# Four-layer graph network on one core: other waits, products and transfer sizes around the node steps

## What is computed

```python
edge_index = jnp.stack([src, dst])
h = jnp.maximum(_layernorm(x, axis=-1), 0.0)
x = x + _L0_gnn_ref(h, node_vec1, src, dst, edge_attr_4, edge_attr_12, ...)
...
x = x + _L2_gnn_ref(h, edge_attr_3, edge_attr_64, ...)
h = jnp.maximum(_layernorm(x, axis=-1), 0.0)
x = x + _L3_gnn_ref(h, node_vec1, edge_attr_4, edge_attr_8, ..., src, dst, 16)
return x
```

```python
skip_s = s @ W_skip0
skip_v = jnp.einsum('nmi,mk->nki', v, W_skip1)
s = s @ W_nl0
v = jnp.einsum('nmi,mk->nki', v, W_nl1)
w = jax.nn.relu(edge_feature @ W_fc1) @ W_fc2
xs = s[dst]
xv = v[dst]
...
tp = jnp.concatenate([out0a, out0b, ...], axis=-1)
agg = jax.ops.segment_sum(tp, src, num_segments=N) / DENOM
out_s = agg_s @ W_out_s + skip_s
out_v = jnp.einsum('nmi,mk->nki', agg_v, W_out_v) + skip_v
```

## Time and profile before

| | us |
|---|---|
| median of three runs | 5989.67 |
| the profiled execution | 5993.88 |
| its span | 5992.1 |
| PE busy | 4809.9 (80%) |
| DVE busy | 4674.1 (78%) |
| POOL busy | 4116.6 (69%) |
| ACT busy | 3747.7 (63%) |
| DMA traffic | 488.43 MB, mean 82 GB/s |

### The profile page before, as it was taken

The page is one execution under the profiler, slowest core; times in us unless marked ns, Lnnn a source line. Parts: engine busy times, 40 slices in busy tenths (PEclk is TensorE's granted clock), DMA queues, the critical chain, the costliest instruction groups (busy, mean ns, idle before and its releaser), DMA issues. The chain is left out here.

```text
span 5992.1 us, 143928 instructions
## 1 busy us (share of the span) xinstructions
PE 4809.9 (80%) x37273; PEld 4178.0 (70%) x37273; DVE 4674.1 (78%) x14217; ACT 3747.7 (63%) x13000; POOL 4116.6 (69%) x4263
## 2 busy tenths in 40 slices
PE   0078787777788888888889899999999878888886
PEld 0047777777777777777777688888888757777775
DVE  9947777777777777777776499999999569999996
ACT  0046666666665666666665477777777468888884
POOL 1677777777777777777777377777776247777772
PEclk9999999999999999999999899999999879999998
DMA  6432333333333333333333233333333223333332
GB/s 195 112 83 72 75 74 76 75 75 75 75 80 82 76 75 75 76 73 75 74 81 77 81 82 81 81 81 80 82 81 76 72 70 84 84 84 85 82 80 62
DMA packets 599937, 488.43 MB, mean 82 GB/s; under 512 B 308280, under 2 KB 526134, under 8 KB 599447
## 3 DMA queue, kind: packets, MB, share of 16 engines
q0 software_dynamic: 195056, 322.11, 21.1%
q1 hardware_dynamic: 366138, 137.90, 10.0%
q10 hardware_dynamic: 38637, 27.25, 1.5%
HBM read 410.81 MB, written 75.56 MB: 81 GB/s over the span
## 5 line engine op out<-in xcount | busy, mean ns | idle before, releaser
L896 PE MATMUL PS<-WK 128*128 128x123 f32 (+1 forms) x21632 | 2677.5, 283 | 264.8 <-issue 208.3
L896 PEld LDWEIGHTS PS<-WK 128*128 128x128 f32 (+1 forms) x21632 | 2565.5, 196 | 443.7 <-issue 416.9
L1136 ACT ACTIVATE WK<-WK 128x64 f32<-128x64 f32 x9984 | 2470.9, 336 | 308.2 <-DVE WK L1601 302.8
L657 POOL DMA_INDIRECT WK<-HT,WK x2080 | 2024.0, 973 | 807.3 <-issue 702.4
L657 POOL DMA_INDIRECT ACC<-HT,WK x832 | 801.3, 963 | 254.8 <-issue 242.4
L576 POOL DMA_INDIRECT TB<-WK x718 | 719.9, 1003 | 247.2 <-issue 233.1
L1105 ACT ACTIVATE WK<-PS 100x512 f32<-100x512 f32 x420 | 246.9, 588 | 689.4 <-PE PS L862 686.2
L879 PE MATMUL PS<-F,WK 100*128 100x192 f32 x3360 | 657.5, 339 | 11.8 <-DVE WK L1619 9.2
L879 PEld LDWEIGHTS PS<-F,WK 100*128 100x128 f32 x3360 | 541.0, 191 | 68.2 <-DVE WK L1619 40.7
L884 PE MATMUL PS<-F,WK 64*128 64x224 f32 (+1 forms) x3360 | 413.3, 365 | 161.2 <-DVE WK L1619 131.5
L657 POOL DMA_INDIRECT WOA<-HT,WK x416 | 425.2, 1022 | 169.7 <-issue 118.9
(11 more groups left out here) (234 smaller groups left out, 6606.2 us busy)
## 6 DMA issues: line engine op xcount, KB each, us to landing
WK<-TA SPq DMA_DIRECT2D x638, 72.0 KB, 1.9
WK<-HT,WK POOLq DMA_INDIRECT x2080
WK<-TB SPq DMA_DIRECT2D x214, 144.0 KB
WK<-in_ea SPq DMA_DIRECT2D x23, 612.0 KB
TA<-WK POOLq DMA_DIRECT2D x23, 612.0 KB, 7.6
ACC<-HT,WK POOLq DMA_INDIRECT x832
WK<-in_eb SPq DMA_DIRECT2D x400, 32.0 KB
HT<-WK ACTq DMA_DIRECT2D x153, 76.9 KB
```

Of the source, the lines that this page charges most:

```text
L657: eng.indirect_dma_start(out=GB[l][u % 4][:, t, :], out_offset=None, in_=HT[:, :], in_offset=bass.IndirectOffsetOnAxis(ap=idx[:, t, vc:vc ...
L896: m = eng.matmul(psA[q][0:ch, k * BN:(k + 1) * BN], ms[:, t, k * ch:(k + 1) * ch], OH[q][:, t, :], start=(t == 0), stop=(t == G - 1))
L1136: m = eng.activation(m4[:, t, 96 + vb * c:160 + vb * c], m4[:, t, 96:160] if l == 2 else TW[l][q][:, t, :], ACT.Copy, scale=tb[:, t, y1 + ...
```

## The change

- **Waits.** In the edge loops PE's feature transposes, its first edge product (layers 2 and 3) and its sum of messages wait on fewer semaphores.
- **Products of layer 2.** In `mnode` four products of 64, 96, 96 and 96 columns become two of 192 columns. 32 zero columns are put between the two scalar weights, and the second product overwrites what they leave.
- **Filling products.** In the last ten tiles of the node steps 1 to 2 and 2 to 3, where `mout` has no tile left, PE multiplies the identity by output weights (`warm`). Nothing reads the result.
- **Clearing.** Layer 0's `ACC` is cleared in 51 pieces by ACT during node step 0 (`first`).
- **TB.** 166 columns in the prologue, 96 in node step 0 to 1, 120 in node step 1 to 2 (before 174, 104, 104).
- **Skip rows.** Pieces of four tiles in four buffers in place of eight in two.
- **SP.** The eight first loads of layer 3 are issued between the stores of tiles 2, 5, ..., 23, not ahead of all.
- **Start of layer 3.** The evacuation buffers of that node step lie elsewhere (`EV3`), and DVE no longer waits for the last store before it splits layer 3's first features.
- **POOL.** In layers 0 and 1 a group's gathers are issued ahead of its scatter, and the wait on `e.A` moves with them.
- Two semaphores of the prologue's sort are merged into others.

The diff, cut:

```diff
-SB0, SB1 = 174, 104
+SB0, SB1, SB2 = 166, 96, 120
...
-NEV, SKB = 5, 8
+NEV, SKB, NSK = 5, 4, 4
...
-        EVL = [EV0, EV1, EV2, EV2]
-        SK = [WK[0:BN, 4480 + i * SKB * 192:4480 + (i + 1) * SKB * 192].rearrange("p (j d) -> p j d", j=SKB) for i in range(2)]
+        EV3 = [WK[0:BN, 5848 + i * 352:6200 + i * 352] for i in range(NEV)]
+        EVL = [EV0, EV1, EV2, EV3]
+        SK = [WK[0:BN, o:o + SKB * 192].rearrange("p (j d) -> p j d", j=SKB) for o in (3328, 4096, 4864, 7616)]
...
-        loads += [(WS[2][:, 0:64], w["L2_gnn_W_nl0"]), (WS[2][:, 64:160], w["L2_gnn_W_skip0"])]
+        loads += [(WS[2][:, 0:64], w["L2_gnn_W_nl0"]), (WS[2][:, 96:192], w["L2_gnn_W_skip0"])]
...
                 if l == 3:
-                    for u in range(8):
-                        load(0, u)
                     for j in range(NB):
                         store(eng, 3, j)
+                        if j % 3 == 2 and j < 24:
+                            load(0, j // 3)
...
+            eng.memset(WS[2][:, 64:96], 0.0).then_inc(s_wz, 1)
...
                     eng.wait_ge(s_bl[u % 4], i * 64 + (u // 4 * 32 + 64 * NT0 * l + 32))
                     eng.sem_inc(s_sep, 1)
-                    if u % 2 == 0:
-                        follow(i, u)
                     place(TB, lambda q: st[:, q, POSC:POSC + 1].bitcast(I32), st, s_bs[u % 4])
 
                 eng.wait_ge(s_az, l + 1)
                 if l < 2:
                     with eng.Fori(0, NT0) as i:
                         for u in range(8):
+                            gather(i, u, u % 2 == 0)
                             scatter(i, u)
-                            gather(i, u)
                 with eng.Fori(NT0 if l < 2 else 0, n) as i:
                     for u in range(8):
...
-                        eng.dma_start(SK[q % 2][:, 0:w, :],
+                        eng.dma_start(SK[q % NSK][:, 0:w, :],
                                       SC[q * SKB * BN:(q * SKB + w) * BN, 0:192].rearrange("(j p) d -> p j d", p=BN))\
-                           .then_inc(s_sk[q % 2], 16)
...
                     eng.wait_ge(s_le, 3)
-                    skip_rows(0)
-                    skip_rows(1)
+                    for q in range(NSK):
...
                     m = p["nch"] * BN
                     for j in range(NB):
                         eng.wait_ge(s_oo, l * NB + j + 1)
                         x = eng.memset(ACC[:, j * m:(j + 1) * m], 0.0)
-                        if j and j % SKB == 0 and j + SKB < NB:
+                        if j and j % SKB == 0 and j + (NSK - 1) * SKB < NB:
                             eng.wait_ge(s_o, j)
-                            skip_rows(j // SKB + 1)
+                            skip_rows(j // SKB + NSK - 1)
                     x.then_inc(s_az, 1)
...
-                        eng.matmul(o[:, 0:64], t[0:64, 0, 0:BN], WS[2][:, 0:64], start=True, stop=True)
-                        eng.matmul(o[:, 160:256], t[0:64, 0, 0:BN], WS[2][:, 64:160], start=True, stop=True)
-                        eng.matmul(o[:, 64:160], t[0:96, 1, 0:BN], KV[2][:, 0:96], start=True, stop=True)
-                        m = eng.matmul(o[:, 256:352], t[0:96, 1, 0:BN], KV[2][:, 96:192], start=True, stop=True)
+                        s2 = o[:, 0:320].rearrange("p (a f) -> p a f", a=2)[:, :, 0:96]
+                        v2 = o[:, 64:448].rearrange("p (a f) -> p a f", a=2)[:, :, 0:96]
+                        eng.matmul(s2, t[0:64, 0, 0:BN], WS[2][:, :], start=True, stop=True)
+                        m = eng.matmul(v2, t[0:96, 1, 0:BN], KV[2][:, :], start=True, stop=True)
...
+                def warm(t):
+
+                    if lo == 2:
+                        eng.wait_ge(s_o, min(NB, t - 3))
+                    else:
+                        eng.wait_ge(s_xo, lo * NB + min(NB, t - 3))
+                    eng.matmul(psO[t % 4][0:BN, 0:WO[lo].shape[2]], ident[0:ch, 0:BN], WO[lo][:, 0, :], start=True, stop=True)
...
+                        elif lo:
+                            warm(t)
...
-                    if not isinstance(i, int) or g >= 2:
+                    if isinstance(i, int) and g >= 2 or not isinstance(i, int) and (l < 2 or k == 0):
                         eng.wait_ge(e.E, i * 8 + (g - k))
-                    if l >= 2 and (not isinstance(i, int) or g >= 4):
-                        eng.wait_ge(e.S, i * 8 + (g - k - 2))
+                    if l >= 2 and isinstance(i, int) and g >= 4:
+                        eng.wait_ge(e.S, g - k - 2)
...
-                    eng.wait_ge(e.E, i * 8 + (g - q + 2 if l >= 2 else g + 1))
-                    if not (isinstance(i, int) and g - (q if l >= 2 else 0) == 0):
-                        eng.wait_ge(e.S, i * 8 + (g - q if l >= 2 else g))
-                    eng.sem_inc(s_sep, 1)
+                    if l < 2 or isinstance(i, int):
+                        eng.wait_ge(e.E, i * 8 + (g - q + 2 if l >= 2 else g + 1))
+                        if not (isinstance(i, int) and g - (q if l >= 2 else 0) == 0):
+                            eng.wait_ge(e.S, i * 8 + (g - q if l >= 2 else g))
+                        eng.sem_inc(s_sep, 1)
...
                 def edge_a(i, u):
                     q = u % 2
                     ms = MS[l][q][:, 0:G * nm].rearrange("p (t f) -> p t f", t=G)
-                    eng.wait_ge(e.M, i * 8 + (u + 9))
                     eng.wait_ge(e.N, i * 8 + (u + 9))
                     eng.wait_ge(e.V, i * 8 + (u + 2))
...
                     eng.wait_ge(s_oo, lo * NB + j + 1)
                     m = LAYERS[lo]["nch"] * BN
+                    x = eng.activation(ACC[:, j * m:(j + 1) * m], ZERO[:, :].to_broadcast([128, m]), ACT.Copy)
+                    if j == NB - 1:
+                        x.then_inc(s_az, 1)
+
+                def first(j):
+                    if j == 0:
+                        eng.wait_ge(s_ws, 1)
+                        eng.wait_ge(s_px[0], 16)
+                        eng.wait_ge(s_px[1], 16)
+                        eng.wait_ge(s_wz, 6)
+                    m = LAYERS[0]["nch"] * BN
                     x = eng.activation(ACC[:, j * m:(j + 1) * m], ZERO[:, :].to_broadcast([128, m]), ACT.Copy)
                     if j == NB - 1:
                         x.then_inc(s_az, 1)
...
+                    if lo is None and t < NB:
+                        first(t)
...
-            eng.wait_ge(s_px[0], 16)
-            eng.wait_ge(s_px[1], 16)
-            eng.wait_ge(s_wz, 5)
-            m = NB * LAYERS[0]["nch"] * BN
-            eng.activation(ACC[:, 0:m], ZERO[:, :].to_broadcast([128, m]), ACT.Copy).then_inc(s_az, 1)
...
-                        eng.wait_ge(s_sk[j // SKB % 2], 16 * (j // SKB // 2 + 1))
+                        eng.wait_ge(s_sk[j // SKB % NSK], 16 * (j // SKB // NSK + 1))
                         if j >= 2:
                             eng.wait_ge(s_xo, base + j - 1)
-                        eng.tensor_tensor(OO[j % 2], o[:, 0:192], SK[j // SKB % 2][:, j % SKB, :], ALU.add).then_inc(s_o, 1)
...
                     eng.wait_ge(s_xn, NB * (l + 1))
-                    for x in range(NEV):
-                        eng.wait_ge(s_hd[x], all_stored(l)[x])
                     if l == 3:
                         v(eng.memset(twf[:, 0:576], 0.0))
                         w_()
+                    else:
+                        for x in range(NEV):
+                            eng.wait_ge(s_hd[x], all_stored(l)[x])
```

More of the change, by code:

```diff
@@ L279, in program @@
         s_oo, s_xo, s_wz, s_wo, s_ox, s_tl = (sem(n) for n in ("s_oo", "s_xo", "s_wz", "s_wo", "s_ox", "s_tl"))
-        s_sk, s_ske, s_skl = [sem(f"s_sk{i}") for i in range(2)], sem("s_ske"), sem("s_skl")
+        s_sk, s_ske, s_skl = [sem(f"s_sk{i}") for i in range(NSK)], sem("s_ske"), sem("s_skl")
         s_o, s_sg, s_hz = sem("s_o"), sem("s_sg"), sem("s_hz")
@@ L709, in _ @@
             eng.wait_ge(s_cf, 1)
-            eng.matmul(psO[2][:, 0:1], ONE, CF, start=True, stop=True).then_inc(s_cg, 1)
+            eng.matmul(psO[2][:, 0:1], ONE, CF, start=True, stop=True).then_inc(s_cp, 1)
             for b in range(NKEYS):
```

28 lines of the change are left out of this document (15 added, 13 removed).

## The result

The changed kernel is slower: 6012.05 us in the median of 17 runs (5999.98 to 6018.2), beside 5995.88 us for the kernel before in as many (5982.89 to 6000.08). The ratio is 1.0026 with a 95% interval of 1.0019 to 1.0034. Forecast were 5955 us and a gain. The profiled execution took 6011.65 us.

What follows compares the result with a forecast made beforehand. POOL's DMA issue was taken to bound layers 0, 1 and 3, and PE layer 2, leaving gains in prologue and node steps: -11 - 2 - 10 + 0 - 12 = -35 us, giving 5955 us against the median; range 5925 to 5978.

Steps and rivals of the forecast that it cites:

- new order of gather and scatter: Edge loops of layers 0 and 1: worth nothing, 0 us, since POOL issues as many DMAs at the same pace.
- The slower rival: Node step 2 to 3: more skip-row pieces in flight stall SP's stores, giving 6001 us; chance 0.05.
- Prologue: Start of layer 0: clearing in pieces and fewer TB columns start it near 428, not 439; -11 us (-13 to -7).
- Node step 0 to 1: Between layers 0 and 1: 8 fewer TB columns let the stores land a little sooner; -2 us (-3 to 0).
- Node step 1 to 2: Between layers 1 and 2: merged products save 0.44 to 0.48 us a tile, partly limited by ACT's stores; -10 us (-18 to 0).
- stores and loads swallow the node steps: Rival, node steps: ACT's queue limits step 1 to 2, loads take back step 2 to 3's head gain; 5970 us, chance 0.24.
- the clock holds: Rival, last ten tiles: filling products keep PE at full clock, saving up to 10 us; 5945 us, chance 0.07.
- Layer 2: Layer 2's edge loop: removing PE's waits gains 0 us, at the far end 32 us.
- waits were dear: Rival, layer 2: removing PE's waits gains 32 us as well, giving 5924 us; chance 0.11.
- Node step 2 to 3 and layer 3: From layer 2's end into layer 3: smaller skip pieces and an earlier DVE start give -12 us (-25 to +5).
- The head: Start of node step 2 to 3: four-tile skip pieces land after 9 to 11 us, not 19; -9 us (-13 to -3).
- SP's queue is full: Node step 2 to 3: SP's stores bind, so layer 3's interleaved loads add 8 us (0 to +10).

Runs made afterwards that it cites:

- f1: The changed kernel with POOL's scatter put back ahead of the gathers in layers 0 and 1: 5960.08 us, 0.9939 of the kernel before.
- f2: The kernel before with only the gathers put ahead of the scatter in layers 0 and 1: 6042.28 us, ratio 1.0077.
- f3: The changed kernel, gathers still first, with SP's staging slots issued one table load later: 5969.5 us, ratio 0.9952.
- f4: The changed kernel with the scatter first again and PE's removed edge-loop waits put back: 5966.7 us.
- e1: The changed kernel with the scatter ahead of the gathers again, on a chip where the kernel before takes 9043.49 us: 8849.05 us, ratio 0.9792.
- loads-first runs: Changed kernel, scatter first, layer 3's eight loads ahead of all stores again, two runs on slow chips: 8951.39 and 8924.55 us, ratios 0.9811 and 0.9826.
- e2: The kernel before with only the gathers put ahead of the scatter, on a chip where the kernel before takes 9043.49 us: ratio 1.0341.
- short store: Changed kernel, scatter first, storing 16 of 123 skip rows a tile in node step 1 to 2, three slow-chip runs: ratios 0.9804, 0.9828, 0.9779.

## Why the prediction was wrong

**The step that failed** is a sentence of the first part: the new order of gather and scatter is "worth nothing", because POOL issues as many DMAs as before at the same pace. The count was right. What it left out is who waits for the scatter. SP does, for 723.4 us in 1200 before the change (shown above, and in none of the rows that I predicted from), and with SP its whole queue, in which the next table load stands. I had followed the moved scatter on its own engine and at the block of line 925, not on the queue that waits for its landing. Term: 0 forecast, 52 us measured (f1), 26 us a layer, with a price of 44 us on the kernel before (f2: 6042.28 against 5998.32). It took the result to 6012.05 us, past the upper bound of 5978, and to the side that I had given 0.03.

No rival of mine had this mechanism. The slower rival, skip rows starving SP's stores, did not happen: the longest store fell to 5.50 us.

**Prologue**: -14.4 us measured, -11 forecast, of which 1.3 is the border (the scatter that no longer leads). The pieces of the clear cost nothing where I took 2 us: DVE's last instruction of node step 0 starts at 421.62, and at 421.88 before. And the landing came earlier than the 426 that I had called the best case: DVE starts layer 0 at 424.98, released by the last store into `HT`. With the scatter first (f1) POOL starts the layer at 428.50 and not at 439.38, 10.9 us sooner. The mechanism was right.

**Node step 0 to 1**: -2.6, forecast -2; 1.3 of it is the border. Right.

**Node step 1 to 2**: +3.4 and not -10. Three terms were off. First, a merged pair takes 0.94 us (3377.69 to 3378.63) and not 0.62. The row of L771 had two products of one shape; here the second has 96 rows to the first one's 64, and PE's weight loads stand 7.1 us in 30 tiles between them, until the longer first product is nearly through. That the change of rows is the reason is my inference. A tile goes from 3.05 to 2.86 us, 0.19 saved and not 0.44. Second, the saving in the first 40 tiles, 7.6 us by that, came out as 2 to 4 us (126.8 and 125.8 us before and in f2; 124.2, 123.7, 122.7 in the changed kernel, f1 and f3) and as nothing in f4 (127.7). ACT stands longer in the issue of its 102 stores, 96.7 to 112.5 us in these four kernels beside 81.0 and 87.6 in f2 and before, and DVE and PE wait for its evacuation. Third, the last ten tiles take 3 to 4 us more. In all four kernels with 120 columns SP's eight loads for layer 2 start 166 us or more after the last gather and so fall beside these tiles; before and in f2 they start at 140 us, ahead of tile 40, and on the 9000 us chips, where the tiles come later, they also fall ahead of it. I had seen that the loads move and priced it at nothing, because the last store comes after them. On chips of 5990 us both readings, ACT's queue and the loads, rest on these rows and on no edit of their own. This is the rival "stores and loads swallow the node steps", for this step alone.

```profile
PEld PS L764 <- issue: 7.1, 30, 0.4
```

**The clock in the last tiles**: with the filling products the granted clock of the last 25 us was 0.69 in the changed kernel and 0.54 in f1, which has the same ones, where it was 0.51 without them:

```profile
3367.00:3392.00 25.00, 18.27 (x45) 10.48 (x43) 2.35 (x10) 5.33 (x12) 0.00 (x0) 0.54 0.30 93
```

On these chips they do not hold it at 2.4 GHz; on those of 9000 us they do (1.00 in e1). I had also misread: the 4.6 idle us of its 25 lie behind the last product. While it still had products, PE was busy all the time in the kernel before, at half clock:

```profile
3378.00:3397.40 19.40, 19.40 (x76) 15.60 (x76) 3.18 (x14) 4.99 (x12) 0.00 (x0) 0.50 0.21 69
```

The Trainium skill's advice ("TensorE: Matmul & The Clock Gate", section "Why this matters for your kernels") is to leave no long idle gaps between bursts. It does not explain this fall: in the 33 us up to it, from 3345, PE's only gap is 0.58 us, and the changed kernel's longest in the last tiles is 1.55 us. Here the measurement decides. What full clock would be worth on the 5990 us chips is not shown; on the others it is nothing, since the stores set the pace of these tiles. The rival "the clock holds" fell.

**Layer 2**: +0.8, forecast 0, and f4 agrees. The rival "waits were dear" fell: the waits taken out here cost nothing that can be seen.

**Node step 2 to 3 and layer 3**: -20.4 us together, forecast -12 within -25 to +5. The head gave 8.0 us (13.55 against 21.55; forecast 9), the start of layer 3 gave 8.8 (forecast 7). The rest of the step kept 3.6 us, where I had charged 8 for the interleaved loads and credited 4 for shorter stalls. The step that failed is "SP's queue is full": in that step SP waits 68.8 us for ACT's evacuation before the change and 62.9 us after it, of which one wait at the head is 29.3 and 31.2, so the eight loads had room, and the loads-first runs put them at nothing. The 3.6 us itself is small beside the spread: from the first skip add to layer 3's first gather it is 172.6 us before and 169.1, 170.5, 172.6 and 171.7 in the changed kernel, f1, f3 and f4. Halved pieces landed sooner, the first was in use 11.0 us after POOL's issue and not 19.0; so here the advice of the Trainium skill for large DMAs ("DMA: Bandwidth & Descriptors", section "Rules for kernel authors") did not decide: four of them were in flight, and what counted was when the first was complete.

**The sum.** Without its one bad part the change is worth what was forecast for it: f1 takes 5960.08 us, the forecast was 5955, and the result of all other parts is -38 us against 5998.32 (the two traces, f1's and that of the kernel before, are 29 us apart; each is of one run). This is luck in part: the prologue and step 2 to 3 gave 12 us more than forecast, and step 1 to 2 gave 13 less. The spread of the forecast's terms was also added up wrong: their ends come to -59 and -2 us, not to -60 and -10.

The fastest kernel here is f1, the change with POOL's old order: 0.9939 of the kernel before.

## What to carry to other kernels

When an asynchronous operation moves, ask not only what its own engine does then but who waits for its landing, and what stands behind that waiter in its queue. An engine that waits 60% of its time looks idle, yet it may have only a few us in hand for the one load that everyone else needs; here there were 3.7, and a shift of 5.0 us used them up and cost 26 us a layer. Put the load ahead of the wait (f3) or the awaited operation first (f1). And a saving on an engine in a pipeline counts only in the tiles that this engine paces: on the 9000 us chips the merged products paid in the first 40 tiles and the short store in the last ten.

## What was not expected of the hardware

The same kernel took 5998.32 us on one chip and 8979.58 to 9151.89 us on three others, over 25 runs there, with the same packet time of the gathers' queue. The sign of the main finding held, but prices did not carry over: the scatter's order alone cost 0.8% on the one (f2) and 3.4% on the other (e2), and node step 1 to 2 took 340 us there and 204 here. One filling product a tile left the clock of the last tiles at 0.54 to 0.69 here and held it at 1.00 there.
